# The low halves of the activated feed-forward product: all on VectorE, none on GpSimd

## The chip, the cores and the metric

One core of one Trainium2 chip runs the program. The metric is the device time of one execution in microseconds; before the change the median of three runs is 825.43 us (823.97 to 826.21).

## The reference

Eight sequences of 512 tokens with 256 features pass through one transformer block whose RMS norms are scaled and shifted by a condition, and then through a layer norm with a conditional bias:

```python
n  = gamma * rmsnorm(x) + beta                      # gamma, beta, alpha: products of the condition
x  = x + alpha_a * (softmax(scale * q k^T) v) @ W_o.T      # 16 heads of 16
h  = gamma2 * rmsnorm(x) + beta2
x  = x + alpha_f * ((silu(h @ gate_w.T) * (h @ hidden_w.T)) @ out_w.T + out_b)   # 1024 hidden
out = layernorm(x) * weight + bias + tanh(cond @ lin_w.T + lin_b)
out = out * weight + bias
```

## The kernel before

All matrix products of projections and of the feed-forward part are split: each operand is a high half (rounded to fp32r) and a low half (operand minus high half), and three products, high by high, low by high and high by low, are summed in PSUM. So each activation that feeds a product is turned into two tiles.

The work is a hand-written software pipeline. Every engine has a function `unit(n)`, called for n = 0 to `LAST`, and each holds its part of unit n. A batch element b takes 16 units (`UNITS`: four head groups of four 128-token tiles), `u = n % 16` is the place in this round, and `NU` = 128 units hold all attention. In a unit TensorE makes two score products (`scores`, L1134), two score products for the row maxima of eight units ahead (`max_scores`, L1119, into the one bank pair `ps_m`), the product with v (L1147), one job of the table `SCHEDULE` (projections, transposes; L1064, L1070, L1095, L1102), the gate and hidden products of one eighth of a half batch element (`gate_hidden`, L1167) and the output product of the one two units back (`project_out`, L1182). These last two belong to feed-forward step `e = n - 28`, of 128 in all (`NE`). By the table the job is MT, TR, FT, Q, K, MT, WO, WO, MT, FT, V, Q, K, MT, V, TR for u = 0 to 15 (MT: transpose of maxima, TR: of normalised x, FT: of the feed-forward norm, WO: output projection).

The feed-forward step e goes through these instructions: ACT makes tanh of the gate half (`tanh`, L749), DVE two instructions (`gate`: L936, then L943 writes `act_y`), ACT the high half (`a_high`, L756, in unit n + 1 behind the first exponential), and then the low half `a_lo = act_y - a_hi` is made by `a_low`: for e below `TAIL` = 100 by POOL (L472), for the last 28 by DVE (L949). The three places of `act_y` and the four of `a_hi` and `a_lo` are reused, so `gate` waits for the low half of three steps before, and `a_low` for `f_done`, the output product of four steps before.

DVE in unit n: the two row maxima (`reduce_max`, L897, each needed before TensorE may write `ps_m` again), the scaling of a finished feed-forward half (L908, u = 6 and 14), the job's copy (`evac`: L866 for Q and K, L871 for TR, L879 for FT, L886 for MT, L912 for WO), a reciprocal (L918, u = 2 and 11), layer norm statistics (L927, L930; u = 9 and 15), then `a_low(e - 1)` if it is DVE's, then `gate(e)`.

POOL in unit n, in order: at u = 0 `moments` and `normalise` (L530, L430, L432, L540), at 1 `weigh` (L549, L552), at 4 and 13 `o_norm` (L480, waits for a DMA that starts from the reciprocal), at 9 and 12 `norm2` (L430, L432, L507: fx), at 10 `moments`, `normalise` and `root1`; then `a_low` of step `n - 29`; then at u = 0 and 2 `n_low` (L445), at 3 and 10 `n2_low` (L523), at 5 and 14 `o_low` (L485), at 6, 7, 8 and 14 `add_to_x` (L496), at 9 and 13 `add_bias` (L516), at 11 `weigh`, at 1 and 15 `v_copy` (L453). Each waits for its operands, and what stands behind waits with it.

Of the kernel before, what the change touches and what calls it, by code (L numbers as in the profile page):

```python
# [5 lines left out]
F32 = mybir.dt.float32  # L6
F32R = mybir.dt.float32r
ALU = mybir.AluOpType
# [28 lines left out]
NE = 2 * B * JC  # L37
TAIL = NU - GH_AT
# [30 lines left out]
def build(nc, dram):  # L69
    with ExitStack() as ctx:  # L70
        def sb(name, shape, dt=F32):
            return ctx.enter_context(nc.sbuf_tensor(name, shape, dt))
# [4 lines left out]
        def sem(name):  # L77
            return ctx.enter_context(nc.semaphore(name))
# [38 lines left out]
        act_y = sb("act_y", [P, 3, HT])  # L117
        a_hi = sb("a_hi", [P, 4, HT], F32R)
        a_lo = sb("a_lo", [P, 4, HT], F32R)
# [53 lines left out]
        sq2 = sem("sq2"); rstd2_r = sem("rstd2_r"); fx_r = sem("fx_r"); bias_r = sem("bias_r")  # L173
        n2_hi_r = sem("n2_hi_r"); yf_r = sem("yf_r"); n2_lo_r = sem("n2_lo_r")
        gh_full = sem("gh_full"); t_r = sem("t_r"); s_r = sem("s_r"); y_r = sem("y_r")
        a_hi_r = sem("a_hi_r"); a_lo_r = sem("a_lo_r"); a_tail_r = sem("a_tail_r"); f_done = sem("f_done")
        stat_r = sem("stat_r"); mv_r = sem("mv_r"); centre_r = sem("centre_r"); rstd3_r = sem("rstd3_r")
        z_r = sem("z_r"); z_last_r = sem("z_last_r"); out_w = [[sem(f"out_w{h}{u}") for u in range(2)] for h in range(2)]

# [232 lines left out]
        def _(pool):  # L412
# [51 lines left out]
                    hi, lo = (a[:, rows].rearrange("p j n -> p (j n)") for a in (ow_hi, ow_lo))  # L464
                pool.tensor_tensor(lo, piece[:, w % 4], hi.bitcast(F32), ALU.subtract).then_inc(piece_lo, 1)

            def a_low(e):

                pool.wait_ge(a_hi_r, e + 1)
                if e >= 4:  # L470
                    pool.wait_ge(f_done, e - 3)
                pool.tensor_tensor(a_lo[:, e % 4, :], act_y[:, e % 3, :], a_hi[:, e % 4, :].bitcast(F32), ALU.subtract)\  # L472
                    .then_inc(a_lo_r, 1)

            def o_norm(b, c):

                k = 2 * b + c
                pool.wait_ge(oc_in, 16 * (k + 1))
                pool.wait_ge(rec_in, 16 * (k + 1))
                pool.tensor_tensor(o_c[:], o_c[:], d_c[:], ALU.mult).then_inc(omul_r, 1)  # L480

            def o_low(b, c):

                pool.wait_ge(ohi_r, 2 * b + c + 1)
                pool.tensor_tensor(on_lo[:, c, :], o_c[:], on_hi[:, c, :].bitcast(F32), ALU.subtract).then_inc(olo_r, 1)  # L485
# [40 lines left out]
            def moments(b, h):  # L526

                hf = 2 * b + h
                pool.wait_ge(mv_r, 2 * (hf + 1))
                pool.tensor_scalar(centre[:], mv[:, :, 0], -1.0, None, ALU.mult).then_inc(centre_r, 1)  # L530
                root(rstd3[:], mv[:, :, 1], EPS_LN, rstd3_r)

            def normalise(b, h):

                hf = 2 * b + h
                pool.wait_ge(centre_r, hf + 1)
                pool.wait_ge(rstd3_r, hf + 1)
                for t in range(2):
                    xs = xr[:, b % 2, 2 * h + t]
                    pool.tensor_scalar(xs, xs, centre[:, t:t + 1], rstd3[:, t:t + 1], ALU.add, ALU.mult).then_inc(z_r, 1)  # L540
# [29 lines left out]
            def unit(n):  # L570
                b, u = n // UNITS, n % UNITS
                e = n - GH_AT - 1

                def at(k, d):
                    return u == k and 0 <= b + d < B

                if at(0, -3) and b - 3 < B - 1:
                    moments(b - 3, 1)
                    normalise(b - 3, 1)
                if at(1, -3) and b - 3 < B - 1:  # L580
                    weigh(b - 3, 1)
                if at(4, -1):
                    o_norm(b - 1, 1)
                if at(9, -1):
                    norm2(b - 1, 0)
                if at(10, -2):
                    moments(b - 2, 0)
                    normalise(b - 2, 0)
                if at(10, 2):
                    root1(b + 2)  # L590
                if at(12, -1):
                    norm2(b - 1, 1)
                if at(13, 0):
                    o_norm(b, 0)
                if 0 <= e < TAIL:
                    a_low(e)
                if PIECE_AT <= n < PIECE_AT + PIECES:
                    piece_low(n - PIECE_AT)
                if at(0, 1):
                    n_low(b + 1, 0)  # L600
                if at(1, 0) and b > 0:
                    v_copy(b, 3)
                if at(2, 1):
                    n_low(b + 1, 1)
                if at(3, -2):
                    n2_low(b - 2, 1)
                if at(5, -1):
                    o_low(b - 1, 1)
                if at(6, -2):
                    add_to_x(("F", 2 * (b - 2)))  # L610
                if at(7, -1):
                    add_to_x(("WO", 0, b - 1))
                if at(8, -1):
                    add_to_x(("WO", 1, b - 1))
                if at(9, -1):
                    add_bias(b - 1, 0)
                if at(10, -1):
                    n2_low(b - 1, 0)
                if at(11, -2):
                    weigh(b - 2, 0)  # L620
                if at(13, -1):
                    add_bias(b - 1, 1)
                if at(14, 0):
                    o_low(b, 0)
                if at(14, -2) and n < LAST - JC:
                    add_to_x(("F", 2 * (b - 2) + 1))
                if at(15, 1):
                    for g in range(NG - 1):
                        v_copy(b + 1, g)
# [227 lines left out]
        def _(dve):  # L857
# [74 lines left out]
            def gate(e):  # L932

                bank = gh_bank(e)
                dve.wait_ge(t_r, e + 1)
                dve.scalar_tensor_tensor(out=gate_t[:, e % 2, :], in0=gate_t[:, e % 2, :], scalar=1.0, in1=bank[:, 0:HT],  # L936
                                         op0=ALU.add, op1=ALU.mult).then_inc(s_r, 1)
                dve.wait_ge(s_r, e + 1)
                if 3 <= e < TAIL + 3:
                    dve.wait_ge(a_lo_r, e - 2)  # L940
                elif e >= TAIL + 3:
                    dve.wait_ge(a_tail_r, e - 2 - TAIL)
                dve.tensor_tensor(act_y[:, e % 3, :], bank[:, HT:T], gate_t[:, e % 2, :], ALU.mult).then_inc(y_r, 1)  # L943

            def a_low(e):

                dve.wait_ge(a_hi_r, e + 1)
                dve.wait_ge(f_done, e - 3)
                dve.tensor_tensor(a_lo[:, e % 4, :], act_y[:, e % 3, :], a_hi[:, e % 4, :].bitcast(F32), ALU.subtract)\  # L949
                   .then_inc(a_tail_r, 1)  # L950

            def last_norm():

# [46 lines left out]
            def unit(n):  # L1000
                b, u = n // UNITS, n % UNITS
                e = n - GH_AT

                def at(k, d):
                    return u == k and 0 <= b + d < B

                if n == 0:
                    evac(("TR", 0, 1))
                if n + JC < NU:
                    reduce_max(2 * (n + JC))  # L1010
                if n + JC < NU:
                    reduce_max(2 * (n + JC) + 1)
                if at(6, -2):
                    scale(("F", 2 * (b - 2)))
                if at(14, -2):
                    scale(("F", 2 * (b - 2) + 1))
                if job_at(n) and n < NU:
                    evac(job_at(n))
                if at(2, -1):
                    o_recip(b - 1, 1)  # L1020
                if at(11, 0):
                    o_recip(b, 0)
                if at(9, -2):
                    statistics(b - 2, 0)
                if at(15, -2) and b - 2 < B - 1:
                    statistics(b - 2, 1)
                if TAIL <= e - 1 < NE:
                    a_low(e - 1)
                if 0 <= e < NE:
                    gate(e)  # L1030
                if job_at(n) and n >= NU:
                    evac(job_at(n))
# [6 lines left out]
        def _(pe):  # L1039
# [131 lines left out]
            def project_out(e):  # L1171

                hf, j = e // JC, e % JC
                if e < TAIL:
                    pe.wait_ge(a_lo_r, e + 1)
                else:
                    pe.wait_ge(a_tail_r, e - TAIL + 1)
                if j == 0 and hf > 0:
                    pe.wait_ge(sc_r, SC_NO["F", hf - 1])
                for t in range(2):  # L1180
                    for m, (a, c) in enumerate(PARTS):
                        mm = pe.matmul(ps_f[:, t, :], A[a][:, e % 4, t * P:(t + 1) * P], OW[c][:, j, :],  # L1182
                                       start=(j == 0 and m == 0 and t == 0), stop=(j == JC - 1 and m == 2),
                                       skip_group_check=True)
                mm.then_inc(f_done, 1)
# [112 lines left out]
```

## Time and profile before

| | |
|---|---|
| median of three runs | 825.43 us |
| profiled execution, its own time | 824.8 us |
| its span | 823.0 us |
| mean granted TensorE clock | 0.973 |

The busy share of PE, DVE, ACT and POOL is 90, 65, 59 and 46% of the span. TensorE falls short mainly in the first 180 us and in the last 80. In the profile PE is a matrix product, PEld the load of its stationary operand, L12 a line of the kernel, and times are microseconds unless marked ns. A mean over a group covers stages with different limits, so what one instruction more on DVE is worth has to be read unit by unit.

### The profile page before, as it was taken

To read this page: it belongs to the slowest core of one execution; us is meant where nothing else is said; L and a number is where in the kernel's file an instruction comes from. 1 tells how busy PE (TensorE), PEld (TensorE's weight loads), DVE (VectorE), ACT (ScalarE), POOL (GpSimd) and SP (SyncE) were. 2 spreads that over 40 slices of the span, in tenths; PEclk is the share of its full clock that TensorE was granted. 3 is DMA by queue.
4 is the path that set the end of the run, shared out by engine and by line. 5 is a ranking of instruction groups with operands and counts; after the bars stand their busy time and mean duration, and the time that the engine had idled before them with its cause. 6 is when DMAs were issued, how large, how long until landed. Compare 5 with 4: busy or idle time off the path is not lost.

```text
span 823.0 us, 14349 instructions
## 1 busy us (share of the span) xinstructions
PE 744.5 (90%) x5110; PEld 487.3 (59%) x5110; DVE 534.2 (65%) x776; ACT 483.8 (59%) x865; POOL 380.6 (46%) x478
## 2 busy tenths in 40 slices
PE   2778788789998999899998999999998999898896
PEld 2423233346666667566666667566666666568895
DVE  3396666766766676667766676767766676325675
ACT  3326775767666665656666665666556665663332
POOL 4202431343237453566336453465336453574753
PEclk9859998999999999999999999999999999999999
DMA  6663655535430644235430544234440531022010
GB/s 183 214 223 109 206 171 165 191 114 169 128 120 28 207 120 164 81 124 159 132 129 28 202 123 163 83 122 139 122 137 28 194 111 35 29 65 81 14 27 27
DMA packets 61568, 100.17 MB, mean 122 GB/s; under 512 B 10320, under 2 KB 17928, under 8 KB 61496
## 3 DMA queue, kind: packets, MB, share of 16 engines
q1 hardware_dynamic: 60280, 97.99, 37.5%
q10 hardware_dynamic: 1088, 1.05, 0.5%
q8 instruction: 41, 0.67, 0.4%
q14 instruction: 31, 0.25, 0.1%
q0 software_dynamic: 128, 0.20, 0.1%
HBM read 59.60 MB, written 39.09 MB: 120 GB/s over the span
## 4 chain that ended last, share of the span: by engine, by line
PE 57%; issue 13%; DVE 9%; ACT 8%; POOL 7%; DMA 4%; SPq 1%; POOLq 0%; ACTq 0%; DVEq 0%
PE ps_x L1167 14%; PE ps_j L1064 10%; PE ps_s L1134 8%; PE ps_o L1147 8%; PE ps_x L1182 7%; PE ps_m L1119 6%; DVE mx L897 4%; ACT prob L727 4%; DMA ks<-stack_scratch 1%; POOL fx L507 1%; DVE gate_t L936 1%; DVE act_y L943 1%; POOL on_lo L485 1%; POOL a_lo L472 1%; ACT junk L649 1%
## 5 line engine op out<-in xcount | busy, mean ns | idle before, releaser
L727 ACT ACTIVATE prob<-ps_s 128x1024 f32<-128x1024 f32 x256 | 262.0, 1023 | 103.7 <-PE ps_s L1134 103.2
L897 DVE TENSOR_REDUCE mx<-ps_m 128x2 f32<-128x1024 f32 x220 | 269.3, 1224 | 72.8 <-PE ps_m L1119 67.3
L472 POOL TENSOR_TENSOR a_lo<-act_y,a_hi 128x256 fp32r<-128x256 f32 x100 | 73.3, 733 | 164.8 <-ACT a_hi L756 164.8
L1134 PE MATMUL ps_s<-qs,ks 64*128 64x512 f32 x512 | 130.2, 505 | 19.7 <-ACT prob L727 17.7
L1134 PEld LDWEIGHTS ps_s<-qs,ks 64*128 64x128 f32 x512 | 48.6, 186 | 153.8 <-ACT prob L727 129.7
L1147 PE MATMUL ps_o<-prob,v 128*32 128x512 f32 x1024 | 139.2, 616 | 0.0
L1167 PE MATMUL ps_x<-n_hi,gh_hi 128*128 128x256 f32 x436 | 127.1, 292 | 1.3 <-POOL n_lo L523 1.3
L1167 PE MATMUL ps_x<-n_hi,gh_lo 128*128 128x256 f32 x436 | 121.8, 279 | 0.0
L1167 PE MATMUL ps_x<-n_lo,gh_hi 128*128 128x256 f32 x436 | 121.7, 279 | 0.0
L1119 PE MATMUL ps_m<-ks,qs 64*128 64x512 f32 x440 | 100.9, 455 | 15.5 <-DVE mx L897 8.5
L749 ACT ACTIVATE gate_t<-ps_x 128x256 f32<-128x256 f32 x109 | 41.9, 384 | 94.0 <-PE ps_x L1167 93.9
L936 DVE SCALAR_TENSOR_TENSOR gate_t<-gate_t,ps_x 128x256 f32<-128x256 f32 x109 | 45.2, 414 | 73.2 <-ACT gate_t L749 73.2
L1167 PEld LDWEIGHTS ps_x<-n_hi,gh_hi 128*128 128x128 f32 x436 | 82.1, 188 | 4.9 <-issue 4.0
L1167 PEld LDWEIGHTS ps_x<-n_hi,gh_lo 128*128 128x128 f32 x436 | 82.2, 188 | 1.0
L1167 PEld LDWEIGHTS ps_x<-n_lo,gh_hi 128*128 128x128 f32 x436 | 82.0, 188 | 0.0
L1182 PE MATMUL ps_x<-ow_hi,a_hi 128*128 128x256 f32 x256 | 72.3, 282 | 0.8 <-DVE a_lo L949 0.7
L1182 PE MATMUL ps_x<-ow_hi,a_lo 128*128 128x256 f32 x256 | 72.0, 281 | 0.0
L1182 PE MATMUL ps_x<-ow_lo,a_hi 128*128 128x256 f32 x256 | 71.6, 280 | 0.0
L756 ACT ACTIVATE a_hi<-act_y 128x256 fp32r<-128x256 f32 x128 | 52.6, 411 | 29.0 <-DVE act_y L943 29.0
L1119 PEld LDWEIGHTS ps_m<-ks,qs 64*128 64x128 f32 x440 | 42.7, 190 | 41.5 <-DVE mx L897 33.3
L496 POOL TENSOR_TENSOR xr<-xr,sc 128x512 f32<-128x512 f32 x31 | 40.5, 1308 | 26.0 <-DVE sc L908 16.8
L1182 PEld LDWEIGHTS ps_x<-ow_hi,a_hi 128*128 128x128 f32 x256 | 48.0, 188 | 1.6 <-DVE a_lo L949 0.9
(156 smaller groups left out, 1283.8 us busy)
## 6 DMA issues: line engine op xcount, KB each, us to landing
stack_scratch<-qk_hi SPq DMA_DIRECT2D x64, 256.0 KB, 3.3
qs<-stack_scratch SPq DMA_DIRECT2D x32, 512.0 KB, 4.2
ks<-stack_scratch SPq DMA_DIRECT2D x32, 512.0 KB, 5.1
stack_scratch<-qk_lo SPq DMA_DIRECT2D x32, 256.0 KB, 3.6
out_scratch<-o_raw SPq DMA_DIRECT2D x32, 256.0 KB, 2.4
xa<-in_x SPq DMA_DIRECT2D x8, 512.0 KB, 4.0
o_c<-out_scratch SPq DMA_DIRECT2D x16, 256.0 KB
d_c<-reciprocal_scratch SPq DMA_DIRECT2D x16, 256.0 KB
```

Source lines behind the costliest of these rows:

```text
L472: pool.tensor_tensor(a_lo[:, e % 4, :], act_y[:, e % 3, :], a_hi[:, e % 4, :].bitcast(F32), ALU.subtract)\
L727: act.activation(prob[:, n % 2, 2 * h:2 * h + 2, :], ps_s[:], ACT.Exp, scale=SCALE).then_inc(p_r, 1)
L749: act.activation(gate_t[:, e % 2, :], gh_bank(e)[:, 0:HT], ACT.Tanh, scale=0.5).then_inc(t_r, 1)
L756: act.activation(a_hi[:, e % 4, :], act_y[:, e % 3, :], ACT.Copy).then_inc(a_hi_r, 1)
L897: dve.tensor_reduce(mx[:, group % 2, :, h, qt], max_pair(mp)[:], AX.X, ALU.max).then_inc(mx_red, 1)
L936: dve.scalar_tensor_tensor(out=gate_t[:, e % 2, :], in0=gate_t[:, e % 2, :], scalar=1.0, in1=bank[:, 0:HT], op0=ALU.add, op1=ALU.mult).the ...
L1064: mm = pe.matmul(out, lhs(a, k), rhs(c, k), start=(n == 0), stop=(n == len(steps) - 1))
L1119: mm = pe.matmul(max_pair(mp)[:, s, :], qs[r:r + 64, g, j, qt * P:(qt + 1) * P], ks[r:r + 64, g, j, :], start=True, stop=True)
L1134: mm = pe.matmul(ps_s[:, s, :], ks[r:r + 64, g, j, kb * P:(kb + 1) * P], qs[r:r + 64, g, j, :], start=True, stop=True)
L1147: mm = pe.matmul(ps_o[32 * i:32 * i + 32, :], v[:, g, kb, i, :], prob[:, n % 2, i, :], start=(kb == 0), stop=(kb == TT - 1), skip_group_ch ...
L1167: mm = pe.matmul(bank[:, HT * i:HT * (i + 1)], GH[a][:, k, i, j * P:(j + 1) * P], N2[c][:, hf % 2, k, :], start=(m % 6 == 0), stop=(m % 6 ...
L1182: mm = pe.matmul(ps_f[:, t, :], A[a][:, e % 4, t * P:(t + 1) * P], OW[c][:, j, :], start=(j == 0 and m == 0 and t == 0), stop=(j == JC - 1 ...
```

## The change

POOL's `a_low` and its call go. DVE's `a_low` is called for every step, and the two semaphores `a_lo_r` and `a_tail_r` become one.

```diff
@@ pool
-            def a_low(e):
-
-                pool.wait_ge(a_hi_r, e + 1)
-                if e >= 4:
-                    pool.wait_ge(f_done, e - 3)
-                pool.tensor_tensor(a_lo[:, e % 4, :], act_y[:, e % 3, :], a_hi[:, e % 4, :].bitcast(F32), ALU.subtract)\
-                    .then_inc(a_lo_r, 1)
-
...
-                if 0 <= e < TAIL:
-                    a_low(e)
@@ vector
-                if 3 <= e < TAIL + 3:
+                if e >= 3:
                     dve.wait_ge(a_lo_r, e - 2)
-                elif e >= TAIL + 3:
-                    dve.wait_ge(a_tail_r, e - 2 - TAIL)
...
             def a_low(e):
 
                 dve.wait_ge(a_hi_r, e + 1)
-                dve.wait_ge(f_done, e - 3)
+                if e >= 4:
+                    dve.wait_ge(f_done, e - 3)
                 dve.tensor_tensor(a_lo[:, e % 4, :], act_y[:, e % 3, :], a_hi[:, e % 4, :].bitcast(F32), ALU.subtract)\
-                   .then_inc(a_tail_r, 1)
+                   .then_inc(a_lo_r, 1)
...
-                if TAIL <= e - 1 < NE:
+                if 0 <= e - 1 < NE:
                     a_low(e - 1)
@@ tensor
-                if e < TAIL:
-                    pe.wait_ge(a_lo_r, e + 1)
-                else:
-                    pe.wait_ge(a_tail_r, e - TAIL + 1)
+                pe.wait_ge(a_lo_r, e + 1)
```

## Rows read from the trace of the kernel before

**Rows 1.** The page, part 1: busy us, share of the span, instructions.

```profile
PE 744.5 (90%) x5110; PEld 487.3 (59%) x5110; DVE 534.2 (65%) x776; ACT 483.8 (59%) x865; POOL 380.6 (46%) x478
```

**Rows 2.** Busy time by engine, 180 to 740 us; last the clock and DMA.

```profile
core 0: us, PE busy (x) PEld busy (x) DVE busy (x) ACT busy (x) POOL busy (x), PEclk, DMA share, GB/s
180.00:740.00 560.00, 543.19 (x3846) 359.11 (x3848) 371.46 (x545) 354.32 (x622) 280.58 (x356) 1.00 0.38 119
```

**Rows 3.** Waits, 200 to 740 us: total us, times, longest.

```profile
POOL a_lo L472 <- ACT a_hi L756: 158.7, 60, 5.5
...
DVE gate_t L936 <- ACT gate_t L749: 66.2, 72, 3.5
...
PEld ps_m L1119 <- DVE mx L897: 25.4, 82, 1.0
...
PE ps_j L1102 <- POOL fx L507: 9.0, 6, 1.8
```

**Rows 4.** In order of time: unit 84 (u = 4); start, us, instruction, [idle before].

```profile
502.03 0.69 DVE L866 TENSOR_TENSOR qk_lo<-ps_j,qk_hi 128x512 fp32r<-128x512 f32 x1 [1.00 <-ACT qk_hi L690]
...
503.22 0.42 DVE L936 SCALAR_TENSOR_TENSOR gate_t<-gate_t,ps_x 128x256 f32<-128x256 f32 x1 [0.50 <-ACT gate_t L749]
...
504.18 1.23 DVE L897 TENSOR_REDUCE mx<-ps_m 128x2 f32<-128x1024 f32 x1
...
505.46 0.19 PEld L1119 LDWEIGHTS ps_m<-ks,qs 64*128 64x128 f32 x2 [0.22 <-DVE mx L897]
```

**Rows 5.** The same, unit 86 (u = 6).

```profile
514.04 0.69 DVE L912 TENSOR_TENSOR sc<-ps_j,tab_a 128x512 f32<-128x512 f32 x1 [1.40 <-POOL xr L496]
...
514.65 0.41 DVE L936 SCALAR_TENSOR_TENSOR gate_t<-gate_t,ps_x 128x256 f32<-128x256 f32 x1
...
515.43 1.22 DVE L897 TENSOR_REDUCE mx<-ps_m 128x2 f32<-128x1024 f32 x1
...
516.70 0.19 PEld L1119 LDWEIGHTS ps_m<-ks,qs 64*128 64x128 f32 x2 [0.43 <-DVE mx L897]
```

**Rows 6.** Groups by line: the low halves on POOL and on DVE.

```profile
L472 POOL TENSOR_TENSOR a_lo<-act_y,a_hi 128x256 fp32r<-128x256 f32 x100 | 73.3, 733 | 164.8 <-ACT a_hi L756 164.8
...
L949 DVE TENSOR_TENSOR a_lo<-act_y,a_hi 128x256 fp32r<-128x256 f32 x28 | 16.3, 582 | 9.2 <-ACT a_hi L756 8.7 <-PE ps_x L1182 0.5
```

**Rows 7.** In order of time: the tail, POOL and DVE.

```profile
743.99 1.30 POOL L552 TENSOR_TENSOR xr<-xr,tab_b 128x512 f32<-128x512 f32 x1
744.15 1.42 DVE L949 TENSOR_TENSOR a_lo<-act_y,a_hi 128x256 fp32r<-128x256 f32 x1 [0.49 <-ACT a_hi L756]
...
745.49 0.41 DVE L936 SCALAR_TENSOR_TENSOR gate_t<-gate_t,ps_m 128x256 f32<-128x256 f32 x1
...
746.84 0.43 DVE L949 TENSOR_TENSOR a_lo<-act_y,a_hi 128x256 fp32r<-128x256 f32 x1
...
747.19 0.41 DVE L936 SCALAR_TENSOR_TENSOR gate_t<-gate_t,ps_x 128x256 f32<-128x256 f32 x1
```

**Rows 8.** The same, unit 80 (u = 0), POOL and DVE.

```profile
478.41 0.74 POOL L472 TENSOR_TENSOR a_lo<-act_y,a_hi 128x256 fp32r<-128x256 f32 x1
...
479.11 1.29 POOL L445 TENSOR_TENSOR n_lo<-nx,n_hi 128x512 fp32r<-128x512 f32 x1
...
479.36 0.27 DVE L886 SCALAR_TENSOR_TENSOR m_hl<-ps_j,m_hl 16x128 fp32r<-16x128 f32 x1
...
480.24 0.42 DVE L936 SCALAR_TENSOR_TENSOR gate_t<-gate_t,ps_x 128x256 f32<-128x256 f32 x1 [0.61 <-ACT gate_t L749]
480.36 1.28 POOL L549 TENSOR_TENSOR xr<-xr,w 128x512 f32<-128x512 f32 x1
```

**Rows 9.** The same, unit 92 (u = 12), DVE and POOL.

```profile
550.41 0.69 DVE L866 TENSOR_TENSOR qk_lo<-ps_j,qk_hi 128x512 fp32r<-128x512 f32 x1 [1.00 <-ACT qk_hi L690]
...
550.98 1.29 POOL L480 TENSOR_TENSOR o_c<-o_c,d_c 128x512 f32<-128x512 f32 x1 [2.54 <-DMA d_c<-reciprocal_scratch]
```

**Rows 10.** The same, unit 89 (u = 9), POOL and TensorE ahead of fx.

```profile
526.53 0.23 POOL L430 TENSOR_SCALAR rstd<-ss 128x2 f32<-128x2 f32 x1 [1.74 <-ACT junk L649]
...
527.68 1.83 POOL L507 TENSOR_SCALAR fx<-xr,rstd 128x256 f32<-128x256 f32 x2
...
529.65 0.30 PE L1102 MATMUL ps_j<-ident,fx 128*128 128x128 f32 x1 [1.45 <-POOL fx L507]
```

More of the change, by code:

```diff
@@ L175, in build @@
         gh_full = sem("gh_full"); t_r = sem("t_r"); s_r = sem("s_r"); y_r = sem("y_r")
-        a_hi_r = sem("a_hi_r"); a_lo_r = sem("a_lo_r"); a_tail_r = sem("a_tail_r"); f_done = sem("f_done")
+        a_hi_r = sem("a_hi_r"); a_lo_r = sem("a_lo_r"); f_done = sem("f_done")
         stat_r = sem("stat_r"); mv_r = sem("mv_r"); centre_r = sem("centre_r"); rstd3_r = sem("rstd3_r")
```

## The prediction

> **What bounds the kernel now.** I read the page's busy shares first [rows 1], then the same count for the stretch in which POOL makes low halves, 180 to 740 us [rows 2]. There TensorE is busy for 543.19 of 560.00 us at the full granted clock (1.00, the 2.4 GHz level), DVE for 371.46 and POOL for 280.58. So 16.8 us are all that this stretch could give back, and whatever delays TensorE there is lost for good. Next the waits of nearly the same stretch [rows 3]: POOL's largest, 158.7 us, stands before the low halves and costs nothing by itself. TensorE's own loader waits 25.4 us for DVE's maxima (L897), and its product waits 9.0 us, in six pieces, for POOL's fx. DVE waits 66.2 us for ACT's tanh in 72 gates. That stretch holds 96 gates (n = 32 to 127); the other 24 come late, with DVE the last to arrive.
>
> Then one quiet unit in order of time [rows 4]. Its work is Q, and DVE is free at 502.72 (502.03 + 0.69), yet the gate starts at 503.22: 0.50 us are idle. From the gate on nothing is loose: gate, product, maximum (start 504.18, end 505.41), and the loader of the second score product starts at 505.46, having waited 0.22 for that maximum. One bank pair holds both score products of a unit, so the second can't start before the first is reduced. In a unit where another DVE job ends late [rows 5], the gate starts 0.08 before that job's recorded end (514.65 against 514.73), the maximum ends at 516.65, and the loader starts at 516.70 with a wait of 0.43 in place of 0.22. I take from this that DVE time ahead of the gate is free up to the idle time there and is lost one to one beyond it.
>
> **The change, part by part.** POOL loses 100 instructions of 733 ns [rows 6], 73.3 us. TensorE is not waiting for them; they are needed at the end of the following unit. DVE gains 100. What one costs in a queue is its step from start to start: 746.84 to 747.19, 0.35 us [rows 7], and its duration without a collision is 0.43; the mean of the 28 that DVE makes already is 0.58 [rows 6], so some of those collide. It stands between the unit's DVE job and the gate. Its wait on a_hi is satisfied before that (ACT makes a_hi right behind the unit's first exponential, and the unit's maxima come later), and f_done is three units old. While TensorE is full no unit stalls on either, and nothing queued behind the new instruction waits longer for them.
>
> Per round of 16 units, by the DVE job before the gate:
> - Units with idle time of 0.46 us or more (Q, K, maxima, values, and the second output projection): 0.35 fits in [rows 4, 8]. Cost 0. The cover is the wait for tanh; without it the price would be 0.35 each. Unit 11 has 0.26 of idle time and loses 0.01.
> - Four kinds of unit have the gate 0.08 us before the last job's end: unit 2 (feed-forward copy and reciprocal), unit 6 (output scale, rows 5), unit 9 and unit 15 (statistics). In the units that still have score maxima (up to n = 119) I count 6 + 6 + 5 + 5 = 22. 21 of them lose 0.35 and one, which still has slack ahead of its maximum, 0.2: 7.6 us.
> - Units with a transposed copy alone have 0.20 of idle time where the low half needs 0.35 - 0.08 = 0.27: six times 0.07, 0.4 us.
> - From n = 120 on there are no maxima, the gates wait over 2 us for tanh in most units: 0.
>
> That is 8.0 us of plain queueing. To it come collisions with POOL. The low half is the only frequent DVE instruction with both inputs in SBUF. In the tail, POOL's L552 runs from 743.99 to 745.29; DVE's low half, which starts 0.16 later, takes 1.42 instead of 0.43, and the gate behind it starts at 745.49, 0.20 after POOL's end [rows 7]. So a POOL instruction in flight moves the gate to its own end + 0.20. When POOL's operand comes from the same DVE job that precedes the low half, DVE is first and only POOL loses about 0.1. That clears units 1, 2, 6, 7, 9 and 15. Three places are left:
> - Unit 12: POOL's o_norm (L480) starts when a DMA lands, 0.57 after qk_lo starts (550.98 against 550.41), before the low half could (551.02), and ends at 552.27 [rows 9]. Gate at 552.47 instead of 551.60 (1.19 behind qk_lo's start, as in [rows 4]): 0.87. Of five such units, four have L480 in front, by 0.57 to 0.87 each: 2.9 us. The fifth starts 0.47 after DVE is free and is harmless.
> - Unit 3: the same instruction for the other pair. One of them (n = 99) starts 0.06 after DVE is free; since unit 2 now moves DVE 0.35 later against the DMA, it will be 0.29 ahead: 0.7 us.
> - Unit 0: without its low half POOL moves up. L445 takes the place of L472 at 478.41, and L549 follows 1.25 later at 479.66 instead of 480.36 [rows 8]. DVE's low half would start at 479.36 + 0.27 - 0.08 = 479.55, plus 0.35 from unit 15 before it, 479.90: behind L549, which ends at 480.94. Gate at 481.14 where it would have been at 480.24 + 0.35 = 480.59: 0.55. Five rounds: 2.8 us.
>
> Together 6.4 us of collisions. The Trainium skill, SBUF — State Buffer, section "Who interferes with whom", says that a Vector instruction with two SBUF inputs and a GpSimd instruction that reads SBUF exclude each other, and that the loser blocks fully until the other has finished. Read strictly, DVE's whole 0.43 would come behind POOL's end, where the row has it end 0.28 behind; at ten collisions that would make some 1.5 us more than my sum. The row decides.
>
> What can DVE's relief of POOL give back? The 9.0 us for fx are the one target. But the row before fx shows POOL idle for 1.74 us until ACT's squares (L430, then fx until 529.51 and TensorE at 529.65) [rows 10]. No low half lies in that chain, and in the POOL program norm2 precedes the low half of its unit. Gain 0. The last units give and take: the low half of e = 99 meets POOL's normalisation near 741, the next meets POOL's L552 0.7 us earlier than now. I take 0, with 0.7 to either side.
>
> **Sum.** 8.0 + 6.4 = 14.4 us. The profiled execution took 824.8 us (span 823.0), 0.6 under the median of 825.43. So 839.2 against the profiled execution, and 839.8 us against the median.
>
> **Bounds of the unknown terms.** The late-gate price could be 0.43 instead of 0.35 (the duration rather than the step): +1.8. Below, it could be nothing where a later wait for ACT takes it up; the 1.45 us hole at unit 9 can swallow only delay made in unit 8, and there I cost nothing. Collisions: from 0, if DVE wins the close starts, to all 16 of units 0, 3 and 12 at up to 0.9, some 11.
>
> **Rivals.**
> 1. Queueing only. DVE wins where starts are within 0.3 us, or the new rhythm moves POOL out of the way. Unit 12's margins are as small as 0.04 us and unit 0's is 0.24, which speaks for it; the 0.16 of the tail [rows 7] speaks against. 825.4 + 8.0 = 833.4 us.
> 2. Faster: POOL, no longer held by 158.7 us of waits, brings fx earlier. The place is unit 9, the price six waits of 9.0 us in all, giving 816.4 if queueing were also free. It decides from the point where fx is ready when TensorE comes to it, at 528.20 (529.65 less the wait of 1.45); POOL would have to start norm2 that much earlier than ACT's squares allow. Against it: POOL's 1.74 us of idle time [rows 10].
> 3. No change: the one-to-one rule is wrong, since TensorE has other work with which it catches up, and DVE's 65% leaves room. 825.4 us. Against it: the loader's wait is 0.43 in place of 0.22 behind a late gate [rows 4, 5].
> 4. Worse: collisions feed each other (a late unit 12 or 0 brings DVE into the next POOL instruction, at 1.3 us). At 16 collisions of 0.9 and 0.43 for late gates: 825.4 + 9.8 + 14.4 = 849.6 us.
>
> **Numbers.** Forecast 0.62, rival 1 0.22, rival 2 0.04, rival 3 0.06, rival 4 0.06. About 0.3% is what a measurement of this kernel can tell from no change. The range 832 to 845 holds the forecast with its bounds and rival 1 less 1.4 us for a few late gates that are absorbed; rivals 2 to 4 are left out. Faster 0.04 (rival 2), same 0.06 (rival 3), slower 0.90.
>
> **What would show it.** POOL has no L472 and is busy some 307 us; DVE has 128 low halves with a median near 0.43 and a mean clearly above it, about ten of them over 1 us outside the tail. DVE's wait for tanh shrinks by some 30 us. The loader's wait for L897 grows by 8 to 14 us, and TensorE's idle time in the stretch by as much; the holes for fx stay at 1.4 us. Units 2, 6, 9, 15 are 0.35 longer, units 0 and 12 more. It is wrong if the late units don't grow, if the low halves are all 0.43, or if the fx holes shrink.

## The result, and the profile after

The changed kernel takes 839.75 us (median of four runs, 839.48 to 842.03) against 825.82 us for the kernel before, run beside it: a ratio of 1.0171, 95% interval 1.0146 to 1.0197. It is slower, and the forecast was 839.8. The total agrees better than its terms do, as the sections below show; the same kernel measured once more (e8) took 836.5 us, 9.5 above the kernel before beside it, where the sum of the forecast is 14.4.

The page, part 1, of the changed kernel, answering to [rows 1]:

```profile
PE 748.9 (89%) x5110; PEld 489.5 (58%) x5110; DVE 572.3 (68%) x876; ACT 484.5 (58%) x865; POOL 317.1 (38%) x378
```

DVE has 100 instructions and 38 us more, POOL 100 instructions and 63.5 us less, not the full 73.3 (317.1 us are left where I expected some 307). By the groups of lines, POOL's other instructions are 7.0 us longer together (unit 92 below shows one that came behind DVE's low half); the other 2.8 us are overlaps of recorded instructions, which the page counts once. TensorE's idle time, the span less its busy time, grows from 78.5 to 88.8 us. Groups by line, answering to [rows 6]:

```profile
L938 DVE TENSOR_TENSOR a_lo<-act_y,a_hi 128x256 fp32r<-128x256 f32 x128 | 63.5, 496 | 15.4 <-ACT a_hi L746 14.9 <-PE ps_x L1168 0.5
```

Their median is 416 ns. Six of them last over 1 us ahead of the tail, where I expected about ten. The waits of 200 to 752 us, which is the stretch of [rows 3] moved with the work:

```profile
DVE gate_t L926 <- ACT gate_t L739: 36.3, 49, 1.9
...
PEld ps_m L1108 <- DVE mx L887: 36.2, 83, 1.4
...
PE ps_m L1108 <- DVE mx L887: 15.8, 27, 1.1
...
PE ps_j L1091 <- POOL fx L499: 9.0, 6, 1.8
```

DVE's spare time ahead of its gates falls from 66.2 to 36.3 us. TensorE's loader waits 10.8 us longer for the maxima (25.4 before), and TensorE itself 15.8 us where the kernel before has 4.7 between 200 and 740 us (the two overlap and don't add):

```profile
PE ps_m L1119 <- DVE mx L897: 4.7, 9, 0.7
```

TensorE's wait for fx is the same 9.0 us: POOL's relief brought nothing there.

The unit that [rows 5] show, in order of time, first DVE, then the loader:

```profile
522.94 0.69 DVE L902 TENSOR_TENSOR sc<-ps_j,tab_a 128x512 f32<-128x512 f32 x1 [1.41 <-POOL xr L488]
523.55 0.42 DVE L938 TENSOR_TENSOR a_lo<-act_y,a_hi 128x256 fp32r<-128x256 f32 x1
523.88 0.41 DVE L926 SCALAR_TENSOR_TENSOR gate_t<-gate_t,ps_x 128x256 f32<-128x256 f32 x1
524.33 0.42 DVE L931 TENSOR_TENSOR act_y<-ps_x,gate_t 128x256 f32<-128x256 f32 x1
524.67 1.22 DVE L887 TENSOR_REDUCE mx<-ps_m 128x2 f32<-128x1024 f32 x1
...
525.94 0.19 PEld L1108 LDWEIGHTS ps_m<-ks,qs 64*128 64x128 f32 x2 [0.75 <-DVE mx L887]
```

The gate starts 0.94 after the scale, 0.61 before, and the loader's wait grows by the same step, from 0.43 to 0.75. The next fences show unit 80 (u = 0), POOL and then DVE, answering to [rows 8]:

```profile
486.16 1.29 POOL L445 TENSOR_TENSOR n_lo<-nx,n_hi 128x512 fp32r<-128x512 f32 x1
487.41 1.28 POOL L541 TENSOR_TENSOR xr<-xr,w 128x512 f32<-128x512 f32 x1
```

```profile
487.36 0.27 DVE L876 SCALAR_TENSOR_TENSOR m_hl<-ps_j,m_hl 16x128 fp32r<-16x128 f32 x1
487.55 1.43 DVE L938 TENSOR_TENSOR a_lo<-act_y,a_hi 128x256 fp32r<-128x256 f32 x1
488.91 0.41 DVE L926 SCALAR_TENSOR_TENSOR gate_t<-gate_t,ps_x 128x256 f32<-128x256 f32 x1
```

POOL's L541 started 0.14 ahead and ended at 488.69; DVE's low half took 1.43 in place of 0.41, so it ended 0.29 after POOL's end (0.28 in [rows 7]), and the gate came 0.22 after POOL's end. In unit 92 (u = 12), answering to [rows 9], DVE was first:

```profile
560.61 0.42 DVE L938 TENSOR_TENSOR a_lo<-act_y,a_hi 128x256 fp32r<-128x256 f32 x1
561.19 0.42 DVE L926 SCALAR_TENSOR_TENSOR gate_t<-gate_t,ps_x 128x256 f32<-128x256 f32 x1 [0.17 <-ACT gate_t L739]
```

```profile
560.66 1.52 POOL L472 TENSOR_TENSOR o_c<-o_c,d_c 128x512 f32<-128x512 f32 x1 [6.79 <-DMA d_c<-reciprocal_scratch]
```

Here POOL pays, 1.52 in place of 1.29, and the gate is on time.

**A ledger by gates.** The work repeats by unit, so I subtracted the start of each unit's gate in the trace before from that in another trace. The differences step up where time is lost. This table holds the sums in us; the last column is the difference of the spans. Each row compares two single profiles, and a profile can lie up to 3 us from the median of its kernel (e3's took 824.82 us, the shortest of its ten runs, with a median of 827.68), so the steps of the middle column tell more than the last one. The rows below the first two are the experiments of the next section.

| kernel | up to n = 28 | 28 to 120 | 120 to 128 | 128 to 155 | span |
|---|---|---|---|---|---|
| changed | 2.1 | 10.95 | 1.3 | 0.4 | +14.7 |
| changed, again | 2.3 | 10.1 | -0.1 | -0.3 | +12.0 |
| e1, between the maxima | 1.9 | 3.4 | -0.2 | -0.2 | +4.9 |
| e2, late units alone | 0.6 | 7.3 | 1.45 | 2.4 | +11.8 |
| e3, the other units | -0.4 | 1.5 | -0.3 | -0.85 | 0.0 |
| e4, one SBUF input | 0.4 | 7.1 | -0.2 | 2.2 | +9.5 |
| e5, u = 0 moved | 0.2 | 11.2 | 1.3 | -0.6 | +12.1 |
| e6, jobs moved, POOL's low halves | -0.6 | -8.0 | 1.65 | -0.2 | -7.1 |
| e7, jobs moved, DVE's low halves | 1.8 | -1.9 | 1.4 | -0.7 | +0.6 |

In the first profile of the changed kernel, 28 to 120 divides so: the 22 late gates 7.3 us in steps of 0.31 to 0.39; six collisions 4.1 us (four at u = 0 of 0.68 to 0.70, one at u = 12 of 0.72, one at u = 3 of 0.56), of which 0.9 us comes back in the following units in steps of -0.13 to -0.20; the remaining 0.5 us is small steps. The first low half is made at n = 29, so the column ahead of n = 28 is not the work of the low halves.

### The profile page after: what moved, and what is told of

It reads as the page before. It is cut to its first block, busy times and chain, and to the rows that moved or that the text cites. A ratio compares the mean times of both kernels' runs of the same rounds, so it can differ in the third digit from the quotient of the medians.

```text
span 837.7 us, 14349 instructions
## 1 busy us (share of the span) xinstructions
PE 748.9 (89%) x5110; PEld 489.5 (58%) x5110; DVE 572.3 (68%) x876; ACT 484.5 (58%) x865; POOL 317.1 (38%) x378
## 4 chain that ended last, share of the span: by engine, by line
PE 46%; issue 19%; DVE 10%; DMA 9%; POOL 8%; ACT 7%; SPq 1%; POOLq 0%; ACTq 0%; DVEq 0%
PE ps_x L1156 10%; PE ps_j L1053 8%; PE ps_s L1123 7%; PE ps_o L1136 6%; PE ps_x L1168 5%; PE ps_m L1108 5%; DVE mx L887 4%; DMA d_c<-reciprocal_scratch 3%; ACT prob L717 3%; DMA ks<-stack_scratch 2%; POOL fx L499 2%; DMA reciprocal_scratch<-d_s 2%; DVE gate_t L926 1%; POOL o_c L472 1%; POOL on_lo L477 1%
## 5 line engine op out<-in xcount | busy, mean ns | idle before, releaser
L938 DVE TENSOR_TENSOR a_lo<-act_y,a_hi 128x256 fp32r<-128x256 f32 x128 | 63.5, 496 | 15.4 <-ACT a_hi L746 14.9
L477 POOL TENSOR_TENSOR on_lo<-o_c,on_hi 128x512 fp32r<-128x512 f32 x16 | 20.5, 1281 | 135.0 <-ACT on_hi L732 135.0
```

## The experiments

The kernel before, run beside them, had a median of 827.23 us beside e1 to e4 and of 826.99 beside e5 to e8. The expectations below that are times start from about 825.4, so they stand 1.8 and 1.6 us too low for this comparison; the ratios are free of that.

**e1: the low half between the two maxima.** DVE makes all low halves, but in units with score maxima they take the place in which it waits for TensorE's second score product anyway.

```diff
                 if n + JC < NU:
                     reduce_max(2 * (n + JC))
+                    if 0 <= e - 1 < NE:
+                        a_low(e - 1)
                 if n + JC < NU:
                     reduce_max(2 * (n + JC) + 1)
...
-                if 0 <= e - 1 < NE:
+                if 0 <= e - 1 < NE and n + JC >= NU:
                     a_low(e - 1)
```

> All low halves on DVE, but in units with score maxima the low half stands between the two maxima instead of ahead of the gate. In the kernel before DVE waits there 0.6 us in every unit for TensorE's second score product, and a_hi is ready. Queueing theory (DVE time ahead of the gate is what costs): nothing is lost, 825 to 828 us; gates of units 2, 6, 9, 15 start 0.08 us before the last job's end again. Rival (the two engines' exclusion over SBUF is the main cost, wherever the low half stands): 829 us or more. Rival (POOL's freedom shifts its work to worse times): near 835 us.

Measured: 830.25 us, ratio 1.0034 (1.0011 to 1.0056). In the trace of e1, DVE in unit 86, the maxima and what stands between them:

```profile
513.01 1.23 DVE L887 TENSOR_REDUCE mx<-ps_m 128x2 f32<-128x1024 f32 x1
514.17 0.42 DVE L938 TENSOR_TENSOR a_lo<-act_y,a_hi 128x256 fp32r<-128x256 f32 x1
514.84 1.23 DVE L887 TENSOR_REDUCE mx<-ps_m 128x2 f32<-128x1024 f32 x1 [0.24 <-PE ps_m L1110]
```

Even behind the low half 0.24 us of waiting are left. The steps at u = 2 and 6 are gone (0.02 or less) and so are those at u = 0 and 12. The same number of low halves on the same engine costs four fifths less of the ratio (0.0034 for 0.0171; the repeat of the change has 0.0119), so it is the place, not the load. My 825 to 828 was too low, and 830.25 lies where I had put the rival of the exclusion (829 or more). Against 827.23 it is 3.0 us more. Two steps per round are new. At u = 15 the low half waits for POOL's add (1.24 us long in the unit I looked at) and moves the second maximum. At u = 9 it comes when fx is made. POOL in e1, to be held against [rows 10]:

```profile
531.73 2.06 POOL L499 TENSOR_SCALAR fx<-xr,rstd 128x256 f32<-128x256 f32 x2
```

fx takes 2.06 in place of 1.83, and TensorE's wait for it grows from 1.45 to 1.67. Both are collisions of the two engines, one paid by DVE and one by POOL. The ledger's 3.4 us hold 2.5 in these two kinds of step (0.22 to 0.24 each, once 0.49) and one step of 0.73 by the clock (below). So the exclusion, by which one of the two engines is held up as in units 80 and 92 above, costs something here too, but it isn't the main cost.

**e2 and e3: the change in two halves.** e2 gives DVE only the low halves of the units with a late gate, e3 only those of the other units; POOL keeps the rest.

```diff
+def on_dve(k):
+    return k >= TAIL or (0 <= k and (k + GH_AT + 1) % UNITS in (2, 6, 9, 15))
...
-                if 0 <= e < TAIL:
+                if 0 <= e < NE and not on_dve(e):
                     a_low(e)
...
-                if TAIL <= e - 1 < NE:
+                if 0 <= e - 1 < NE and on_dve(e - 1):
                     a_low(e - 1)
```

(e3 has `not in`; the waits for `a_lo_r` and `a_tail_r` count by the same function.)

> The kernel before, except that DVE makes the 22 or 23 low halves of the units whose gate is late already (u = 2, 6, 9, 15); POOL makes the other low halves below step 100. Queueing theory: each costs 0.33 us, 7.4 us in all, so 833 us, with steps at these units alone. Collision theory: few collisions, so under 828 us.

> The complement: DVE makes the low halves of all other units and POOL those of the late ones. Queueing theory: plain queueing costs nothing here and only collisions are left, 1 to 5 us, so 827 to 831 us; steps only where POOL is in flight (unit 12, unit 3; unit 0 only if POOL is still early). If DVE's whole load counted (78 instructions of 0.43), 833 to 860 us.

Measured: e2 835.48 us, ratio 1.0116 (1.0085 to 1.0147); e3 827.68 us, 1.002 (0.9996 to 1.0044). The groups of low halves on DVE, e2 and then e3, from the tiles' view:

```profile
L958 DVE TENSOR_TENSOR a_lo<-act_y,a_hi x53: 361/415/1516, 197.2 to 825.9; 128x256 fp32r<-128x256 f32 x53
```

```profile
L958 DVE TENSOR_TENSOR a_lo<-act_y,a_hi x103: 359/416/1545, 184.6 to 814.1; 128x256 fp32r<-128x256 f32 x103
```

25 more low halves on DVE (53 against 28) cost 7.3 us between n = 28 and 120; 75 more (103) cost 1.5. The steps of e2 stand at u = 2, 6, 9 and 15 and nowhere else (0.28, 0.34, 0.32 and 0.33 each), and none of the 25 added low halves takes over 0.45 us: these steps hold no collision. The time of e2 lies 2.5 us above my 833. The two columns ahead of its last in the ledger hold 3.9 us (e3's hold -1.1), which the part on the clock explains for the most part; but 1.8 of the 2.5 us are the higher kernel before. e3's ratio can't be told from 1. In e3 the steps are two collisions at u = 12 (0.88 and 0.71). u = 0, with four collisions in the changed kernel, has none: unit 15's gate, whose low half is POOL's here, isn't moved, DVE is earlier by that 0.33, and its low half starts 0.10 ahead of L541's counterpart. One of e3's two:

```profile
550.68 1.29 POOL L490 TENSOR_TENSOR o_c<-o_c,d_c 128x512 f32<-128x512 f32 x1 [6.52 <-DMA d_c<-reciprocal_scratch]
```

```profile
550.71 1.54 DVE L958 TENSOR_TENSOR a_lo<-act_y,a_hi 128x256 fp32r<-128x256 f32 x1
552.18 0.41 DVE L946 SCALAR_TENSOR_TENSOR gate_t<-gate_t,ps_x 128x256 f32<-128x256 f32 x1
```

A lead of 0.03 us was enough for POOL there. A recorded lead of 0.01 wasn't: in units 44 and 60 of e3, and in unit 76 of the changed kernel, POOL's instruction behind the DMA starts 0.01 ahead of the low half, takes 1.57, and the low half takes 0.42.

**e4: the load without the second SBUF input.** The kernel before, plus a DVE maximum over act_y at the low half's place.

```diff
                 if TAIL <= e - 1 < NE:
                     a_low(e - 1)
+                if 0 <= e - 1 < TAIL:
+                    dve.wait_ge(y_r, e)
+                    if e - 1 >= 2:
+                        dve.wait_ge(spare_r, e - 2)
+                    dve.tensor_reduce(spare[:, (e - 1) % 2:(e - 1) % 2 + 1], act_y[:, (e - 1) % 3, :], AX.X, ALU.max)\
+                       .then_inc(spare_r, 1)
```

> The kernel before, with all low halves below step 100 on POOL, plus one DVE maximum over act_y (128x256, a single SBUF input, result unused) at the place where the change puts the low half. It does nothing for the output. Queueing theory: 22 late gates by its step of 0.3 to 0.4, 7 to 9 us, so 833 to 835 us, and every gate step the same with no long instructions on DVE. Port theory (the cost comes from the two-input form): no change, 826 us.

Measured: 832.82 us, ratio 1.0086 (1.0055 to 1.0118). The new instruction in its trace, by tile:

```profile
L1034 DVE TENSOR_REDUCE spare<-act_y x100: 360/407/420, 185.4 to 747.7; 128x1 f32<-128x256 f32 x100
```

Its longest is 420 ns, where the low half's longest in the changed kernel is 1435. Only some of the 100 met a long POOL instruction with two SBUF inputs already in flight, at u = 0 and 12 above all. In unit 92, POOL and then DVE:

```profile
555.84 1.29 POOL L481 TENSOR_TENSOR o_c<-o_c,d_c 128x512 f32<-128x512 f32 x1 [2.26 <-DMA d_c<-reciprocal_scratch]
```

```profile
556.17 0.41 DVE L1034 TENSOR_REDUCE spare<-act_y 128x1 f32<-128x256 f32 x1
```

With one SBUF input neither was lengthened. POOL wasn't relieved either. The steps stand where e2 has them: 0.31 at u = 6 and 9, 0.3 at 15, 0.23 at 2 (e2 0.28), together 7.1 us. The median is just under the expected 833 to 835; the ratio's 0.0086 is again 7.1 us. Queueing alone makes this.

**e5: u = 0 out of the way.** The change, with the low half of u = 0 between the maxima.

```diff
                 if n + JC < NU:
                     reduce_max(2 * (n + JC))
+                    if 0 <= e - 1 < NE and u == 0:
+                        a_low(e - 1)
...
-                if 0 <= e - 1 < NE:
+                if 0 <= e - 1 < NE and (u != 0 or n + JC >= NU):
                     a_low(e - 1)
```

> The change, but in units u = 0 with score maxima the low half stands between the two maxima instead of ahead of the gate, where it met POOL's L541. Collision theory: the four steps of 0.70 at n = 48, 64, 80, 96 (and the 0.14 given back behind each) go: 2.2 us less than the change, the rest as it was. Rival (the steps at u = 0 come from POOL's work being early, whatever DVE does): they stay, no difference.

Measured: 835.04 us, ratio 1.0091 (1.0067 to 1.0116). The four steps at u = 0 went, but the ledger's second column didn't fall (11.2): three collisions at u = 12 and three at u = 3 came, of 0.63 to 0.83, where the first profile of the change has one each. Its 835.04 us are 1.5 below the changed kernel measured beside it (836.5), with runs that overlap. The mechanism at u = 0 is confirmed, and the saving that I expected isn't: collisions behind a DMA come and go from run to run.

**e6: the late gates repaired, in the kernel before.** The scaling of u = 6 and the reciprocal of u = 2 move between the maxima of their unit, the statistics of u = 9 and 15 between those of the next.

```diff
                     reduce_max(2 * (n + JC))
+                    if at(6, -2):
+                        scale(("F", 2 * (b - 2)))
+                    if at(2, -1):
+                        o_recip(b - 1, 1)
+                    if at(10, -2):
+                        statistics(b - 2, 0)
+                    if at(0, -3) and b - 3 < B - 1:
+                        statistics(b - 3, 1)
                 if n + JC < NU:
                     reduce_max(2 * (n + JC) + 1)
...
-                if at(6, -2):
+                if at(6, -2) and n + JC >= NU:
                     scale(("F", 2 * (b - 2)))
...
-                if at(9, -2):
+                if at(9, -2) and n + 1 + JC >= NU:
                     statistics(b - 2, 0)
```

(and so for the reciprocal and for u = 15.)

> The kernel before with its low halves on POOL. In units with score maxima, the jobs that make the gate late on DVE move between the two maxima: the reciprocal of u = 2, the feed-forward scaling of u = 6, and the statistics of u = 9 and 15 into the following unit. Queueing theory: the lateness that these units have now goes, 0.2 at each u = 2 and 6, 0.7 at u = 9, 0.3 at u = 15, in all 6 to 8 us: 817 to 821 us, faster than both kernels. Rival (DVE's lateness costs nothing before the change, since TensorE is the bound): no change.

Measured: 817.75 us (816.19 to 820.63), ratio 0.99 (0.9879 to 0.9921): as expected, and faster than both kernels. DVE in the unit of [rows 5]:

```profile
504.53 0.68 DVE L908 TENSOR_TENSOR sc<-ps_x,tab_b 128x512 f32<-128x512 f32 x1
505.21 1.23 DVE L897 TENSOR_REDUCE mx<-ps_m 128x2 f32<-128x1024 f32 x1
506.90 0.69 DVE L912 TENSOR_TENSOR sc<-ps_j,tab_a 128x512 f32<-128x512 f32 x1 [0.46 <-PE ps_j L1072]
...
508.68 0.42 DVE L936 SCALAR_TENSOR_TENSOR gate_t<-gate_t,ps_x 128x256 f32<-128x256 f32 x1 [1.09 <-ACT gate_t L749]
```

The scaling (L908) stands ahead of the second maximum, the output projection's (L912) waits for TensorE and no longer for POOL, and the gate has 1.09 us of idle time ahead instead of none. TensorE's loader waits 17.4 us for maxima between 200 and 740 us, 25.4 before:

```profile
PEld ps_m L1127 <- DVE mx L897: 17.4, 82, 0.2
```

**e7: the same moves with DVE's low halves ahead of the gate.**

> The same moves on the changed kernel (all low halves on DVE, ahead of the gate). Queueing theory: the price of a low half depends on the idle time before its gate, so u = 6 costs nothing now, u = 15 about 0.07, u = 2 and 9 0.2 to 0.35 each: 2 to 4 us of queueing in place of 7.4, and the collisions of 3 us or new ones; so 5 to 8 us above the kernel with the moves alone. If the price is a fixed one per low half, 13 to 15 us above it.

Measured: 825.5 us (822.26 to 830.65), ratio 0.9991 (0.9974 to 1.0008); 7.75 us above e6 by the medians (5 to 8 expected, and 13 to 15 by a fixed price per low half), 6.1 in the second column. The unit that had cost 0.33 in the change costs nothing against e6 (u = 6), u = 15 costs 0.06, u = 9 still 0.33. The price follows the idle time of each gate, not the instruction. Unit 2 costs 0.46, more than forecast, since POOL's n_lo is in flight when the reciprocal no longer stands before the low half. POOL and then DVE in unit 50 of e7:

```profile
305.93 1.61 POOL L515 TENSOR_TENSOR n_lo<-fx,n_hi 128x256 fp32r<-128x256 f32 x2 [3.63 <-DVE fx L869]
```

```profile
306.21 0.72 DVE L938 TENSOR_TENSOR a_lo<-act_y,a_hi 128x256 fp32r<-128x256 f32 x1
```

Unit 1 costs 0.2 that I had not forecast and didn't trace, and two collisions (0.58 at u = 12, 0.69 at u = 3) are in the 6.1 us as well.

**e8: the changed kernel once more.**

> The changed kernel once more, to see which part of the difference repeats: the steps of the gates should repeat to 0.05 us each (12.7 us from n = 28 to the end less what the clock does), while the 2.1 us ahead of n = 28 and the stretch at half clock near 725 us, if they are chance, differ.

Measured: 836.5 us (two runs), ratio 1.0119 (1.0091 to 1.0147). The steps at u = 2, 6, 9 and 15 repeat to 0.03. The collisions don't: two of the four at u = 0, one at u = 12, two at u = 3. The start repeats (2.3 after 2.1), the 1.3 us behind n = 120 doesn't.

**The clock.** Granted clock and busy time by stretches around that place (PE's is the first number, the clock the one ahead of the last two), the changed kernel in its first profile:

```profile
712.00:718.00 6.00, 5.87 (x47) 4.34 (x46) 2.76 (x5) 2.26 (x4) 1.40 (x1) 1.00 0.00 1
718.00:724.00 6.00, 4.00 (x30) 2.42 (x29) 1.37 (x4) 4.59 (x11) 3.20 (x5) 1.00 0.19 54
724.00:730.00 6.00, 5.88 (x34) 4.07 (x33) 3.27 (x10) 3.20 (x8) 3.17 (x6) 0.72 0.13 43
730.00:736.00 6.00, 5.87 (x45) 4.34 (x46) 1.95 (x5) 4.21 (x8) 5.65 (x8) 1.00 0.03 5
```

The mean of 0.72 over 6 us means that TensorE is granted half its clock (the 1.2 GHz level) for 3.4 us, after 2.0 us of idle time in the six before, and the gate of n = 122 loses 1.13 us against the kernel before, 1.39 against the kernel's own repeat. In the kernel before the same hole is there, with 4.00 us of busy time from 706 to 712, and the clock stays at 1.00:

```profile
706.00:712.00 6.00, 4.00 (x30) 2.43 (x30) 1.13 (x3) 4.26 (x12) 4.51 (x7) 1.00 0.14 46
712.00:718.00 6.00, 5.88 (x46) 4.21 (x44) 2.90 (x9) 4.51 (x11) 3.76 (x8) 1.00 0.18 49
```

A step of 1.06 to 1.22 us at n = 122 stands in five traces (changed, e2, e5, e6, e7) and in none of before, e1, e3, e4 and e8. As e8 is the changed kernel itself, the kernel doesn't decide it. e1 has a step of 0.73 at n = 42 of the same kind (granted clock 0.74 and 0.83 in the stretches from 252 to 260 us), and e2 and e4 have over 2 us more in the tail, with a granted clock of 0.62 from 770 to 774 (e2) and 0.72 from 768 to 774 (e4), where the kernel before has 1.00.

## Why the prediction was right, and where it wasn't

- **DVE time ahead of the gate is free up to the idle time and lost beyond it.** Right, and the main cause: 7.3 us measured where I had 7.6 for the 22 late gates. The step is 0.33 rather than 0.35. e2 shows it alone, e4 without POOL, e6 by its reverse, e7 by its dependence on idle time. The transposed copies cost 0.04 to 0.05 instead of 0.07.
- **One to one.** Right for a gate that is late already. For one that was on time and is pushed by 0.7, some 0.14 to 0.20 comes back in the next unit. The term for collisions had to be net of that.
- **Collisions, 6.4 us.** Mis-sized: 3.1 us net in the first profile, and as much a matter of the run. At u = 12 I had four of five; one came in the first profile, one in the repeat, three in e5. In the other four L472 starts between 0.09 us before and 0.01 behind the moment at which DVE's job ends; the low half starts 0.08 before it, level or ahead, and DVE was first. My step took single starts of one profile, with margins from 0.04 to 0.3 us against DMAs, as fixed. At u = 3 the forecast collision came (n = 99) in the change, its repeat and e5, and others joined in the last two. At u = 0 the place and the reason were right, the price 0.70 instead of 0.55 (POOL's L541 starts 0.05 behind the start of DVE's m_hl, where my sum had it 0.05 ahead, and the gate follows 0.22 behind POOL's end), and the fifth (n = 112) didn't come.
- **No gain from POOL's relief.** Right: the wait for fx is 9.0 us before and after. POOL's idle time moved to other waits.
- **The rest, 0 forecast.** 2.1 us ahead of n = 28, 1.3 behind n = 120 and 0.4 later filled just what the collisions left open: 10.95 in place of 14.4 between n = 28 and 120, and 3.7 elsewhere. The 839.8 for 839.75 is in part luck: my sum had no term for TensorE's clock, and this made good what I had put too high for the collisions. The repeat, at 836.5 and 1.2% rather than 1.7%, shows it. Its ledger adds up to 12.0 instead of 14.7: 1.4 less for the clock's step, 0.9 less between n = 28 and 120, 0.7 less in the tail.

Of the rivals, queueing only is what e4 built, 7 us; its claim that DVE wins the close starts held for four of five at u = 12 and for none of four at u = 0 in the first profile, two of four in the repeat. The faster rival fell with the unchanged wait for fx, the rival of no change with e2 and e4, and the worse one with six collisions instead of its sixteen.

**Open.** The 2.1 and 2.3 us ahead of n = 28 repeat in the changed kernel, and e1 and e7, which have all low halves on DVE too, show 1.9 and 1.8; but e5 has them as well and shows 0.2. No instruction of the change runs there. In the changed kernel 1.3 of the 2.1 us arise in one place, between two exponentials of ACT (85.60 us in place of 85.09, and 90.36 in place of 88.53), and the granted clock differs there. Before, and then changed:

```profile
84.00:88.00 4.00, 3.08 (x22) 0.96 (x18) 2.28 (x2) 2.85 (x5) 1.28 (x1) 0.86 0.54 173
```

```profile
84.00:88.00 4.00, 3.31 (x16) 1.17 (x16) 1.62 (x3) 2.65 (x6) 1.08 (x2) 0.50 0.29 95
```

The repeat has 0.50 in this stretch too, e5 has 1.00. So this part goes with the clock as well. It isn't shown what decides the clock, neither here nor after the same hole at n = 122.

## What to carry to other kernels

An engine with 35% of idle time has no room where its queue is late already. Before one instruction is added to every round, list for each kind of round the idle time just ahead of the instruction that the bounding engine waits for, and place the new one in a wait that ends on another engine: between the maxima it was nearly free, ahead of the gate it cost 7 us. Whoever has that list may first repair the late rounds: moving four jobs into the same gap gained 1.0%, while none of the other places and engines tried here for the low halves gained anything.

## What the runs showed of the hardware that I had not expected

- Which engine gets through first isn't told by the recorded starts when the POOL instruction is queued behind another. POOL and then DVE in unit 64 of e8:

```profile
391.92 1.30 POOL L445 TENSOR_TENSOR n_lo<-nx,n_hi 128x512 fp32r<-128x512 f32 x1
393.17 1.70 POOL L541 TENSOR_TENSOR xr<-xr,w 128x512 f32<-128x512 f32 x1
```

```profile
393.31 0.40 DVE L938 TENSOR_TENSOR a_lo<-act_y,a_hi 128x256 fp32r<-128x256 f32 x1
```

  L541 again starts 0.14 ahead of DVE, as in unit 80 of the first profile, but here POOL is the one that is stretched (1.70 in place of 1.28) and the low half takes 0.40. L541's start is recorded before L445's end (393.22); measured from that end the two are 0.09 apart. A start behind a DMA tells more: in e3 a recorded lead of 0.03 went to POOL and leads of 0.01 to DVE.
- The exclusion hurts whoever comes second, and what it costs depends on what waits for the second: at u = 9 in e1 it was POOL's fx, on TensorE's path, that was stretched by 0.23.
- TensorE's clock halved for 3.4 us after a hole in five of the ten traces and not in the others, at a price of 1.1 to 1.2 us against the kernel before. That is nearly as much as four late gates, so single profiles of such kernels have to be compared by stretches and not by their spans.
